# A graph and mixture-of-experts block on one core: the first mixture sorted by choice, the graph layer's scales moved two groups ahead

## The reference, cut to what matters

```python
x = x + gnn0(layernorm(x))     # spectral graph layer (eigenvectors of the 64 x 64 graph)
x = x + ffn0(layernorm(x))     # mixture of 8 experts, the best 2 per token
x = x + gnn1(layernorm(x))     # graph convolutions, then 4 LSTM passes over windows of 1 to 4 nodes
x = x + ffn1(layernorm(x))     # mixture of 8 experts, the best 1 per token

# ffn0, the layer that the change is mostly about
top_w, top_i = top_k(xf @ Wg + bg, 2);  top_w = softmax(top_w)
for e in range(8):
    h = gelu(xf @ W1[e] + b1[e])                 # 128 -> 512
    out += w_dense[:, e] * (h @ W2[e] + b2[e])   # 512 -> 128
# gnn1, its first part
h = relu(adj @ (x @ Wg0 + bg0));  h = relu(adj @ (h @ Wg1 + bg1))
# first LSTM pass, windows of one node: h = sigmoid(o) * tanh(sigmoid(i) * tanh(g))
```

## Time and profile before

| what | value |
|---|---|
| median of 3 runs | 1651.18 us (1650.91 to 1659.6) |
| the profiled execution's own time | 1653.19 us |
| its span, first to last instruction | 1651.4 us |
| mean granted TensorE clock | 0.886 |
| busy, share of the span: PE / PEld / DVE / ACT / POOL | 74 / 53 / 52 / 46 / 36 % |

### The profile page before, as it was taken

How to read it: one execution, slowest core, us unless ns; L and a number is a source line. 1 busy time by engine, 2 the same in 40 slices (tenths; PEclk the granted TensorE clock), 3 DMA queues, 4 the chain that set the end, 5 groups by cost and what they waited for, 6 DMA issues and landing times. The chain is left out here.

```text
span 1651.4 us, 26932 instructions
## 1 busy us (share of the span) xinstructions
PE 1229.3 (74%) x5977; PEld 874.8 (53%) x5978; DVE 860.5 (52%) x3547; ACT 763.9 (46%) x1920; POOL 599.2 (36%) x1015
## 2 busy tenths in 40 slices
PE   2444425487577999999487787999997897667776
PEld 1223314376566999998344343445443453656665
DVE  5777898856583222222466763444444675711111
ACT  3555534321175455545144444656554664633332
POOL 3666335200003556655577730000000000057775
PEclk9999855786589999999689889999999898589999
DMA  9300000001101222223122100000000332222221
GB/s 260 89 1 2 0 1 1 1 1 55 47 0 31 66 69 71 70 68 67 48 50 50 44 23 1 0 0 0 0 0 0 77 76 51 1 63 75 76 74 44
DMA packets 85697, 68.45 MB, mean 41 GB/s; under 512 B 18630, under 2 KB 74511, under 8 KB 85628
## 3 DMA queue, kind: packets, MB, share of 16 engines
q1 hardware_dynamic: 71228, 36.32, 9.0%
q0 software_dynamic: 14400, 31.39, 7.7%
HBM read 41.55 MB, written 26.64 MB: 41 GB/s over the span
## 5 line engine op out<-in xcount | busy, mean ns | idle before, releaser
L1493 POOL DMA_INDIRECT g_Z<-z,sitter x72 | 70.6, 980 | 507.8 <-SPq L1479 480.2
L1398 ACT ACTIVATE c_H<-ps,c_b 128x256 f32<-128x256 f32 x284 | 117.4, 471 | 133.5 <-PE ps L1427 132.6
L1342 POOL DMA_INDIRECT c_Z<-z,c_idx x142 | 138.2, 973 | 81.0 <-POOLq L1340 57.5
L1840 PE MATMUL ps<-BIG,w_ihT 128*128 x364 | 156.4, 579 | 5.2 <-ACTq L1853 5.2
L1628 POOL DMA_INDIRECT d_Y<-y,seat x128 | 130.2, 1017 | 60.7 <-issue 37.5
L1442 PE MATMUL ps<-w_dn,c_H 128*128 x1136 | 139.3, 276 | 3.4 <-ACT c_H L1398 3.0
L1427 PE MATMUL ps<-c_ZT,c_w 128*128 128x256 f32 x568 | 136.3, 383 | 1.4 <-ACT c_ZT L1386 1.4
L1442 PEld LDWEIGHTS ps<-w_dn,c_H 128*128 128x128 f32 x1136 | 132.4, 192 | 5.5 <-issue 5.2
L1840 PEld LDWEIGHTS ps<-BIG,w_ihT 128*128 128x128 f32 x364 | 69.8, 192 | 86.7 <-issue 86.7
L1376 DVE TENSOR_TENSOR c_ys<-ps,b_dn 128x256 f32<-128x256 f32 x71 | 30.2, 425 | 157.8 <-PE ps L1442 157.8
L1545 ACT ACTIVATE g_H<-ps,bias_cols 128x256 f32<-128x256 f32 x144 | 60.4, 471 | 111.2 <-PE ps L1582 110.4
(11 more groups left out here) (510 smaller groups left out, 2760.2 us busy)
## 6 DMA issues: line engine op xcount, KB each, us to landing
y<-c_ys SPq DMA_DIRECT2D x71, 128.0 KB, 1.8
z<-ZB SPq DMA_DIRECT2D x32, 256.0 KB, 2.6
z<-X SPq DMA_DIRECT2D x16, 256.0 KB, 4.2
c_Z<-z,c_idx POOLq DMA_INDIRECT x142, 2.6
w_up<-in_L_ffn_W_dram SPq DMA_DIRECT2D x1, 2048.0 KB
w_dn<-in_L_ffn_W_dram SPq DMA_DIRECT2D x8, 256.0 KB
w_dn<-in_L_ffn_Wd_dram SPq DMA_DIRECT2D x8, 256.0 KB
d_Y<-y,seat POOLq DMA_INDIRECT x128, 2.5
```

Of the source, the lines that this page charges most:

```text
L1342: pool.indirect_dma_start(Z[u][:, h, :], None, z, bass.IndirectOffsetOnAxis(ap=idx[h][u][:, 0:1], axis=0)).then_inc(fetched[u], 16)
L1398: act.activation(H[u][:, c, :], UP[u][c // 2][:, c % 2 * SLOT_TILE:(c % 2 + 1) * SLOT_TILE], ACT.Gelu, bias=(b1[u] if w_up is not None els ...
L1493: pool.indirect_dma_start(Z[t % DEPTH][h][:, :], None, z, bass.IndirectOffsetOnAxis(ap=k.sitter[:, t * HALVES + h:t * HALVES + h + 1], axis=0)
L1840: last = pe.matmul(view(k.ps[4 * u + j], wide, lanes), k.w_ihT[:, w, :], state(i, u, s, p, wide, lanes), start=True, stop=(s == 0))
```

## The change

1. **Sorting by choice.** `route_choices` replaces `route` for the first mixture. The two choices are sorted into two lists of their own, each of `REGION` = 72 blocks of 128 slots (144 blocks, 72 tiles of two blocks). Every block has its own expert. The counts are made by bf16 matmuls of the two one-hot tables. The list loop has 128 steps as before, each with an `ohh` of 72 columns. The numbers of the experts of a tile's two blocks are packed into one word (first x 8 + second), written behind the loop.
2. **First experts** (`experts_in`). Each half of a tile has its own expert: up weights and up biases are copied twice a tile, the up-projection is 8 matmuls of 128 columns, there are 8 gelus of 128 x 128, and the down bias is added in two instructions. POOL's program is written out tile by tile, with the index columns used in place. While the first 36 tiles (first choices) run, POOL also fetches one half of each later tile into `BIG`, from where DVE stages it (`stage`). From tile 41 on, POOL fetches the results of the first choice, and DVE adds them to `X` with `W1`, two token tiles a step (`combine`).
3. **Second graph stage.** Only the second choice's result is fetched and added there (14 buffers). The scales of group g+2 are made in turn g of the loop, their small operations set between the combines and statistics of group g+3 and `new_state(g-2)`. ACT's normalizing of group g+1 is split around the relu and the gates, the tanh is moved to an earlier place, and each gate matmul and each gate signals by itself.
4. The constant `upper` is such that the prefix sum needs no subtraction afterwards (both routings).

```diff
+REGION = -(-((B * N + E * (P - 1)) // P) // 2) * 2
+SLOTS0 = 2 * REGION * P
-AHEAD = 8
+AHEAD = 14
+Y_RING = 8
+def route_choices(nc, k, sem):
...
+            with dve.Fori(0, TILES * n // DEEP) as i:
+                for b in range(DEEP):
+                    t, c = i * (DEEP // n) + b // n, b % n
+                    dve.wait_ge(oh_used, i * DEEP + (b + 1))
+                    ts_(ohh[b][:, :], k.irow[:, c * REGION:(c + 1) * REGION], hi[:, ds(t + c * TILES, 1)], k.token[:, ds(t, 1)],
+                        ALU.is_equal, ALU.mult).then_inc(oh_ready, 1)
...
+            link(stt(out=k.expert[:, 0:REGION], in0=ef[:, ::2], scalar=float(E), in1=ef[:, 1::2], op0=ALU.mult, op1=ALU.add))
+def experts_in(nc, k, sem, z, y):
...
+        def experts_of(eng, t):
+            both = eng.value_load(k.expert[0:1, ds(t, 1)], min_val=0, max_val=E * E - 1)
+            return [both // E, both % E]
...
+            for t in range(2, NT):
+                pool.wait_ge(turned, t - 1)
+                fetch(t, 0)
+                if t < SECOND:
+                    fetch(t, 1)
+                    fetch_ahead(SECOND + t)
+                if t == COMBINE + 1:
+                    for u in range(2):
+                        pool.wait_ge(stored[u], 16 * (SECOND // 2))
+                if t > COMBINE:
+                    for m in range(2):
+                        fetch_result(2 * (t - COMBINE - 1) + m)
...
+            def step(s, j, q, staging, combining):
...
+                    weights(s + 1, 1 - u, None if early else s * PER, None if early else s * PER)
+                if staging and (not known or s + 2 < NT):
+                    stage(s + 2, u)
+                if combining:
+                    for n in range(2):
+                        combine(s * 2 + (n - 2 * COMBINE), 2 * j + n, q - COMBINE // 4 + 1)
+                if not known or s > 0:
+                    biased(s - 1, 1 - u, q * 2 + (j - 1) // 2 if j else q * 2 - 1)
...
+                for c in range(C):
+                    if c % 2 == 0:
+                        act.wait_ge(up, t * PER + (c + 2) * HALVES)
+                    for h in range(HALVES):
+                        o = c % 2 * SLOT_TILE + h * P
+                        act.activation(H[u][:, c, h * P:(h + 1) * P], UP[u][c // 2][:, o:o + P], ACT.Gelu,
+                                       bias=b1[u][h][:, c:c + 1]).then_inc(gelu, 1)
+                if not (isinstance(t, int) and t == NT - 1):
+                    turn_out(t + 1, 1 - u)
...
 # gnn1, DVE
-            for g in range(GROUPS + 3):
+            for g in range(GROUPS + 2):
                 if 1 <= g <= GROUPS:
                     add_bias(g - 1)
+                if g >= 2:
                     new_cell(g - 2)
+                if g + 2 < GROUPS:
+                    scale(g + 2, g + 3, g - 2)
+                elif g >= 2:
+                    new_state(g - 2)
 # gnn1, ACT
+                ahead = 1 <= g < GROUPS - 1
+                if ahead and g > 1:
+                    normalized(g + 1, range(2))
                 if g < GROUPS:
                     act.wait_ge(up, g + 1)
                     act.activation(HT[u][:, :], UP[:, :], ACT.Relu).then_inc(h_ready, 1)
-                if g < GROUPS - 1:
-                    normalized(g + 1)
+                if 1 <= g <= GROUPS:
+                    gate(g - 1, 0)
+                if ahead:
+                    normalized(g + 1, range(2 if g > 1 else 0, 3))
+                if 1 <= g <= GROUPS:
+                    gate(g - 1, 1)
+                    gate(g - 1, 2)
+                if ahead:
+                    normalized(g + 1, range(3, 4))
```

More of the change, by code:

```diff
@@ new lines, in paired @@
+def paired(eng, step, first, stop):
+    with eng.Fori(0, (stop - first) // 2) as i:
+        for j in range(2):
+            step(i * 2 + (first + j), j, i + first // 2, first)
+def experts_in(nc, k, sem, z, y):
+    staged, w_ready, b_ready, turned, turned_sb, up, gelu, dn, y_ready, used = (
+        sem("c_" + n) for n in "staged w b turned turned_sb up gelu dn y used".split())
+    HALVES = SLOT_TILE // P
+    z_in = [[sem(f"c_z{u}{h}") for h in range(HALVES)] for u in range(2)]
+    ahead = [sem(f"c_ahead{n}") for n in range(2)]
+    y_in = [sem(f"c_y{b}") for b in range(Y_RING)]
+    stored = [sem(f"c_stored{u}") for u in range(2)]
@@ L1345, in _ @@
[L1345 to L1439, removed]
-                    for h in range(HALVES):
-                        for c in range(C):
-                            last = pe.matmul(Y[v][:, h * D:(h + 1) * D], H[v][:, c, h * P:(h + 1) * P],
-                                             w2[:, ds(es[h % kinds] * (C * D) + c * D, D)], start=(c == 0), stop=(c == C - 1))
-                    last.then_inc(dn, 1)
-            sweep(pe, step, NT)
@@ L1447, in _ @@
+            for m in range(2 * (NT - COMBINE - 1), TILES):
+                fetch_result(m)
         @block.sync
@@ L1660, in scale @@
-                link.need(got_sum)
-                link(stt(out=k.ga[:, :], in0=k.ga[:, :], scalar=0.25, in1=k.gb[:, :], op0=ALU.mult, op1=ALU.add))
-                inverse_root(dve, link, k, k.ga[:, :], k.rstd[:, r], bits[:, :], half[:, :], root[:, :])
-                stt(out=k.mean[:, r], in0=k.gm[:, :], scalar=-0.5, in1=k.rstd[:, r],
-                    op0=ALU.mult, op1=ALU.mult).then_inc(scaled, 1)
+                link.put(tt_(v, v, v, ALU.mult))
+                rows(1, combine)
+                link.need(got_both + 1)
@@ new lines, in scale @@
+                got = link.put(stt(out=v, in0=v, scalar=0.25, in1=k.gb[:, :], op0=ALU.mult, op1=ALU.add))
+                rows(0, stats)
+                link.need(got)
+                got = link.put(ts_(bits[:, :].bitcast(I32), v.bitcast(I32), 1, None, ALU.logical_shift_right))
+                link.put(ts_(half[:, :], v, -0.5, None, ALU.mult))
+                rows(1, stats)
+                link.need(got)
+                got = link.put(ts_(out.bitcast(I32), bits[:, :].bitcast(I32), -1.0, SEED, ALU.mult, ALU.add))
@@ new lines, in scale @@
+                rows(2, combine)
+                for turn in range(3):
+                    link.need(got)
+                    got = link.put(tt_(t, out, half[:, :], ALU.mult))
+                    if turn == 0:
+                        rows(3, combine)
+                    link.need(got)
+                    got = link.put(tt_(t, t, out, ALU.mult))
+                    if turn == 0:
+                        rows(2, stats)
+                    if turn == 1 and state >= 0:
+                        new_state(state)
+                    link.need(got)
+                    got = link.put(stt(out=out, in0=t, scalar=1.5, in1=out, op0=ALU.add, op1=ALU.mult))
+                    if turn == 0:
+                        rows(3, stats)
@@ L1666, in add_bias @@
+                link.need(got)
+                stt(out=k.mean[:, r], in0=k.gm[:, :], scalar=-0.5, in1=out, op0=ALU.mult, op1=ALU.mult).then_inc(scaled, 1)
             def add_bias(g):
@@ L1704, in _, with normalized @@
         def _(act):
-            def normalized(g):
+            def normalized(g, tiles):
                 u = g % 2
                 act.wait_ge(scaled, g + 1)
-                if g >= 2:
-                    act.wait_ge(mixed, g - 1)
-                for j in range(GT):
+                for j in tiles:
                     n = g * GT + j
```

395 lines of the change are left out of this document (320 added, 75 removed).

## The result

The changed kernel takes 1603.17 us (median of 4 runs, 1599.07 to 1603.7), beside 1651.79 us of the kernel before: a ratio of 0.969, 95% interval 0.9662 to 0.9719. The profiled execution took 1603.22 us with a span of 1601.5, so the spans differ by 49.9 us. Forecast were 28 us less, 1623, and the measured time lies just inside the range. I cut the span where the first instruction of the next stage starts, as in the earlier trace rows: ranking, first list loop, from there to the first fetch, first experts, second graph stage, the rest.

What follows compares the result with a forecast made beforehand. First experts bound by PE, second graph stage by a ring between ACT and DVE. Terms: ranking -5, list loop +11, tail +0.5, second routing -0.6, experts +19, graph stage -53: -28 us, median 1623, range 1600 to 1652.

Steps and rivals of the forecast that it cites:

- the ring: Second graph stage: ACT waits for DVE's `mean`, DVE for ACT's gates, 12.1 us a group; undone, stage -53 us.
- 8.0 from PE's work: Second graph stage: PE's mixings, up-projection, gates and down-projection take 8.0 us a group at full clock.
- 0.2 for the gate: Second graph stage: last gate and one normalizing activation before the next mixing add some 0.2 us, giving 8.2 a group.
- the 5 us for a half clock: Second graph stage: 5 us added for the half clock at its start, 159 to 164 us.
- rival A: First list loop gets the full clock: 16 us less than forecast, 1607 us in total; chance 0.15.
- eight short ones at 0.29 take 2.35: First experts: eight 128-column gelus a tile on ACT take 2.35 us, where four wide ones took 1.59.
- Now PE waits for ACT: First experts: ACT's longer chain sets the tile, 4.05 us for 72 tiles, stage +19 us.
- PE's work a tile is the same: First experts: up-projection with 16 passes of 128 columns in place of 8 of 256 leaves PE's work unchanged.
- B: First experts: lookups decide, splitting costs PE like a second load; tile 4.45 us, total 1652, no change; chance 0.12.
- C: First experts: DVE's copies shut POOL out; tile 4.9 us, 61 us more, total 1684; chance 0.05.
- rival D: Second graph stage: the ring closes again elsewhere, 12.1 us a group, 58 us more, total 1681; chance 0.05.
- 28 instructions at 0.57: Ranking before the first list loop: 28 DVE instructions at 0.57 us each make 16.0 us, -5 us.

## Why the prediction was right, and where it was off

- **The bound and the ring.** Right. The ring from `mean` over the gates and the cell product back to `mean` was what held a group at 12.1 us, and its removal is worth 39 us by the run with the old order. Next in line is PE, as forecast: 8.0 from PE's work and 0.2 for the gate were put down, 7.95 is what a steady group takes, 8.12 is the mean over the fifteen. The 0.2 for the gate and the last normalizing activation was right in kind and low: taking it away gave 0.43 a group. The 8.0 was high: without that wait PE's order takes 7.52. That the sum came within 0.25 of the steady group is luck in part, since the two errors offset each other.
- **Why 63 and not 53.** Four terms: the first bias came 23.5 us after the start in place of 25.4 (829.8 - 806.3), the groups gave 1.2, the end 8.8 us in place of 10.9 (last bias at 951.6), and the 5 us for a half clock were put on top of durations that held it already. I would leave such a term out unless a row shows it beside the others.
- **The list loop.** Right to 0.1 us: 54.57 forecast as 54.5, from the row of the loop with the same shape. The Trainium skill, "TensorE: Matmul & The Clock Gate", section "Why this matters for your kernels", which says that keeping the engine continuously busy brings the full clock, was the other end, rival A. Here PE is busy 54.57 of 54.57 us at 0.50, and in the loops with wider operands 38.63 of 43.00 at 0.96. The measurement decides: PE without a gap stayed at the lower clock here, and the gaps of the wider loops came only after their clock had risen.
- **The first experts: the mis-sized term.** The step "eight short ones at 0.29 take 2.35" failed. A gelu of 128 columns starts each 0.25 us (2.01/8). I had taken the pitch of the Sign activations at the loop's start, another function on another operand, as the price. With 2.01 the chain is 3.79 by the rows, and the half of the old slack (0.05) that I laid on top isn't there. The step behind it stands: ACT's chain is what the tile hangs on as soon as it is longer than PE's work, as the two and four copies show. In the changed kernel it is not longer, so "Now PE waits for ACT" did not come true: PE waits for nobody, and with the copy off ACT the tile stays at 3.79. "PE's work a tile is the same" was wrong by a little: sixteen narrow passes take 16 x 0.1117 = 1.79 us, the eight wide ones 3.74 - 18 x 0.1117 = 1.73, and that is the 0.05 by which the steady tile got longer. With the 72nd tile (3.8) and 71 x 0.05 the stage would be 7.4 longer; 4.7 was measured. Most of the rest lies in uneven tiles, 7.1 us over the steady pace before and 4.9 now, and in a start that is 1.4 us shorter.
- **Lookups and POOL (rivals B and C).** Neither came. PE has no gap before a down-projection in the steady tile, so one load and a split are hidden. The Trainium skill, "SBUF — State Buffer", section "SBUF: two separate sides", says that a DVE copy within SBUF keeps GpSimd from writing descriptors until it ends; the run with more copies shows 0.08 us a tile for 0.8 us of added copies: the sign is as stated, the size a tenth. To this kernel that is 4 us with the copies doubled.
- **Ring closing again (rival D).** It did not: 7.95 a group, and 7.5 with one activation moved.
- **Ranking and tail.** The ranking was forecast with 28 instructions at 0.57; 31 take 0.44 each: the two choices' passes stand one behind the other without a wait, and DVE no longer stands 3.19 us for the fp32 counts, a wait that the 0.57 had in it (the bf16 counts cost none). Behind the loop the expert table costs 2.3 us, just above the bound of 2 that I had set.

The errors of the experts (14 us), the graph stage (10) and the ranking (2) all point the same way, and the tail (1.8) and the rest (3.2) give back some: 28 + 14.3 + 10.2 + 2.4 - 1.8 - 3.2 = 49.9. So 1603 lies outside the forecast's own band of 1610 to 1636 and 4 us from rival A's 1607, though A's full clock did not come. That it is in the range at all is owed to the room left for A, and that is luck.

## What to carry to other kernels

Price an instruction from a row with its own function and operand; a neighbouring one was a seventh off per step, and with eight of them in a chain it made the forecast's largest error. Where two chains in a period come out equally long, the profile can't say which decides: take work out of one in a first run, and lengthen it by a small known amount in a second. And before columns are taken off a matmul in a loop, look up the granted clock of a loop of that shape: here half the columns cost 11 us, and zeros in their place brought them back.

## What was not expected of the hardware

A loop of 128 x 128 weight loads with 72 moving columns ran at 1.2 GHz for its whole 54.6 us with PE never idle; with 108 columns it had a granted clock of 0.96 and was 11.6 us shorter, though each pass did half as much again. Cutting an ACT copy of 256 columns from PSUM into two or four costs only 0.05 and 0.18 us.
